# Mixer stage of a decoder on one core: pair products as a ring, residual between the halves of the next block, feed-forward weights split later

## What is computed

```
# long convolution, 32 heads of 8 channels, along the 512 features; ctx is k and v, x is q
kv[i, j] = ctx[i] * ctx[j]                       # 64 products per head, 36 different pairs
y[i, j]  = causal_convolution(kv[i, j], ssm_kernel[head]) + D[head] * kv[i, j]
out[j]   = sum over i of y[i, j] * x[i]
x = layernorm(x + out)
# feed-forward, 512 -> 1408 -> 512
x = layernorm(x + ((silu(x @ gate.T * gate_s) * (x @ up.T * up_s)) @ down.T) * down_s)
```

## Time and profile before

| | us |
|---|---|
| median of 3 runs | 2226.83 (2217.18 to 2228.21) |
| the profiled execution | 2228.92 |
| its span, first to last instruction | 2227.10 |
| PE busy in the span | 1929.4 (87%) |
| DVE busy | 1296.5 (58%) |
| ACT busy | 907.3 (41%) |
| POOL busy | 353.0 (16%) |
| mixer stage, from its first transpose to its last matmul | 624 to 1304 |

### The profile page before, as it was taken

The page is one execution under the profiler, slowest core; times in us unless marked ns, Lnnn a source line. Parts: engine busy times, 40 slices in busy tenths (PEclk is TensorE's granted clock), DMA queues, the critical chain, the costliest instruction groups (busy, mean ns, idle before and its releaser), DMA issues. The chain is left out here.

```text
span 2227.1 us, 32834 instructions
## 1 busy us (share of the span) xinstructions
PE 1929.4 (87%) x11952; PEld 1535.5 (69%) x11952; DVE 1296.5 (58%) x2794; ACT 907.3 (41%) x2264; POOL 353.0 (16%) x508
## 2 busy tenths in 40 slices
PE   6979999999955988998998867899998578888966
PEld 5869998998834887887888855566665345555543
DVE  3446444444436665555565335677776368888847
ACT  2234333333312422222222123656555368788821
POOL 0000000000023222222221011232323311112001
PEclk9989999999967999999999988999999889999988
DMA  2221000000122311110110121000000276554334
GB/s 97 67 85 48 20 20 20 20 20 20 34 81 76 105 34 29 39 43 24 39 29 15 39 76 38 10 29 29 29 20 20 92 201 160 143 146 123 76 117 138
DMA packets 86255, 136.60 MB, mean 61 GB/s; under 512 B 9481, under 2 KB 25481, under 8 KB 86097
## 3 DMA queue, kind: packets, MB, share of 16 engines
q1 hardware_dynamic: 86096, 134.52, 20.6%
HBM read 79.88 MB, written 21.05 MB: 45 GB/s over the span
## 5 line engine op out<-in xcount | busy, mean ns | idle before, releaser
L1142 PE MATMUL yp<-cc,toep 128*128 128x288 f32 x640 | 184.4, 440 | 28.1 <-ACT ring L940 28.1
L1901 ACT ACTIVATE e_p<-e_s_ps,e_nb 128x512 f32<-128x512 f32 x256 | 175.1, 698 | 54.0 <-DVE e_nb L1949 51.8
L1949 DVE TENSOR_REDUCE e_nb<-e_s_ps 128x2 f32<-128x1024 f32 x128 | 155.8, 1218 | 54.7 <-PE e_s_ps L2026 54.0
L1142 PEld LDWEIGHTS yp<-cc,toep 128*128 128x128 f32 x640 | 127.9, 208 | 65.1 <-ACT ring L940 28.4
L2036 PE MATMUL e_t_ps<-ident,e_p 128*128 128x128 f32 x1024 | 148.6, 284 | 24.6 <-DVE e_pT L1956 13.3
L2036 PEld LDWEIGHTS e_t_ps<-ident,e_p 128*128 128x128 f32 x1024 | 120.8, 147 | 62.0 <-issue 52.5
L954 ACT ACTIVATE sg<-gu_ps,gs_col 128x256 f32<-128x256 f32 x88 | 41.7, 474 | 281.5 <-PE gu_ps L82 281.5
L80 PE MATMUL q_ps<-a_xt_hi,wq_hi 128*128 128x256 f32 x512 | 151.8, 297 | 4.1 <-DVE wo_lo L112 4.1
L1415 ACT ACTIVATE p<-p,nb,rq 128x128 f32<-128x128 f32 (+1 forms) x256 | 137.0, 539 | 37.9 <-DVE nb L1513 37.8
L1047 DVE SCALAR_TENSOR_TENSOR hm<-gu_ps,us_col,sg 128x256 f32<-128x256 f32 x88 | 42.3, 481 | 187.7 <-ACT sg L954 187.7
L883 POOL TENSOR_TENSOR cc<-ct 128x224 f32<-128x224 f32 (+6 forms) x224 | 112.7, 538 | 230.8 <-ACT ct L920 195.9
(11 more groups left out here) (270 smaller groups left out, 5266.7 us busy)
## 6 DMA issues: line engine op xcount, KB each, us to landing
x_after<-n_r SPq DMA_DIRECT2D x24, 512.0 KB, 3.0
toep<-padded_kernels SPq DMA_DIRECT2D x32, 256.0 KB, 3.5
qs<-e_xh SPq DMA_DIRECT2D x64, 128.0 KB, 2.5
qs<-e_xl SPq DMA_DIRECT2D x64, 128.0 KB, 2.6
ks<-e_ch SPq DMA_DIRECT2D x64, 128.0 KB, 2.6
ks<-e_cl SPq DMA_DIRECT2D x64, 128.0 KB, 2.6
x<-x_after SPq DMA_DIRECT2D x12, 512.0 KB, 4.6
x<-in_x SPq DMA_DIRECT2D x8, 512.0 KB, 4.0
```

Of the source, the lines that this page charges most:

```text
L1142: last = pe.matmul(yp[:, lo % 2, 0:NCOL], toep[h % 2][:, (lo - li) * P:(lo - li + 1) * P], cc[h % 2][:, li, :], start=(li == 0), stop=(li ...
L1901: act.activation(pr[i][:, a, :], s_ps[i][:, a, :], ACT.Exp, bias=nb[i][:, a:a + 1], accum_out=sums[t][:, j, q:q + 1]).then_inc(e_done, 1)
L1949: dve.tensor_reduce(nb[i][:], s_ps[i][:], AX.X, ALU.max, negate=True).then_inc(nb_done, 1)
```

## The change

- **Ring of pairs.** The pairs of a head are taken round a ring of eight channels: `ct` and `qt` hold their 64 columns twice, so that pair (i, i + d) is a window that starts d channels on. POOL then needs two instructions (distance 4, and distances 1 to 3 in one), ACT squares as before. The 288 columns lie in `ccy`, and PE's matmuls read them as before.
- **Result in place.** `copy_y` writes the convolved columns back into `ccy`, laid out as windows with their continuation (three copies), so there is no `ys`; `copy_y` no longer waits for `pr_done`, and the products and squares of head h wait for the sums of head h - 2 (`ot_done`). So that this is possible, the unit with output blocks 2 and 3 comes first. `terms` are two instructions, `sums` four, and the partial sums beside them are `low`, in the ring tile. `qt` is copied by heads into three buffers.
- **Order.** `heads_at` moves the products of a head one unit pair later, to the tick before its first unit. POOL does `products` before the powers, ACT `squares` before `copy_c`, DVE `sums` before `pair_statistics`.
- **Early residual.** At step 0 of a block PE does the first half of `turn_x`, `down(m-1, 10)`, the second half, and then the unit. DVE does `finish(m-1)`, without its statistics, between the two halves of `lo_x`; the statistics (`block_statistics`) stay in step 1.
- **Later weights.** Six pieces in the opening (at odd ticks), then three in each step of block 0.

```diff
-ct = sb("ct", [P, LB, P])
-qt = [sb(f"qt{k}", [P, LB, P]) for k in range(2)]
+ct = sb("ct", [P, LB, 2, 2, HB])
+qt = [sb("qt0", [P, LB, 2, HB]), sb("qt1", [P, LB, 2, HB]),
+      core.ring[:, 3 * D:4 * D].rearrange("p (k r n) -> p k r n", k=LB, r=2)]
...
-cc = [sb(f"cc{k}", [P, LB, NCOL]) for k in range(2)]
-ys = core.ring[:, 3 * D:3 * D + LB * NCOL].rearrange("p (k n) -> p k n", k=LB)
-pr = sb("pr", [P, HI, LB, HB])
+ccy = [sb(f"ccy{k}", [P, LB, XCOL]) for k in range(2)]
+low = core.ring[:, 4 * D:4 * D + LB * 3 * HB].rearrange("p (k r n) -> p k r n", k=LB, r=3)
...
+def around(tile, first, step, count):
...
+    whole = tile if len(tile.ap) == 3 else tile.rearrange("p k r n -> p k (r n)")
+    start = whole[:, :, first:first + 1]
+    return bass.AP(tensor=start.tensor, offset=start.offset,
+                   ap=[list(start.ap[0]), list(start.ap[1]), [step, count], [1, HB]])
...
 def pieces(m, j, t):
...
     if m is None:
-        return range(t, t + 1)
-    return range(UP + 2 * j, min(UP + 2 * j + 2, len(split.pieces))) if m == 0 else range(0)
+        return range(t // 2, (t + 1) // 2) if t else range(0)
+    return range(UP // 2 + 3 * j, min(UP // 2 + 3 * j + 3, len(split.pieces))) if m == 0 else range(0)
...
 def heads_at(t):
...
-    return (t + 3) // 2 if t % 2 and t <= 2 * HC - 5 else None
+    return (t + 1) // 2 if t % 2 and 3 <= t <= 2 * HC - 3 else None
...
     def _(pool):
         def products(h):
...
+            p = h // 2
+            c, out = ct[:, :, h % 2, :, :], ccy[h % 2]
...
+                pool.wait_ge(ot_done, h - 1)
...
+            pool.tensor_tensor(out[:, :, 0:HB // 2], c[:, :, 0, 0:HB // 2], c[:, :, 0, HB // 2:HB], ALU.mult)
+            pool.tensor_tensor(out[:, :, HB // 2:HB // 2 + 3 * HB].rearrange("p k (r n) -> p k r n", r=3),
+                               around(c, 0, 0, 3), around(c, 5 * B, B, 3), ALU.mult).then_inc(cc_done, 1)
...
         for m, j, t in schedule():
+            if t is not None and heads_at(t):
+                products(heads_at(t))
+            if t is not None and t % 4 == 3 and t >= 7:
+                pair_power((t - 7) // 4)
...
-            if t is not None and t % 4 == 3 and t >= 7:
-                pair_power((t - 7) // 4)
-            if t is not None and heads_at(t):
-                products(heads_at(t))
...
+                act.wait_ge(sq_done, 2 * p)
+            act.activation(ct[:].rearrange("p k h r n -> p (k h) r n"),
+                           tr[:].rearrange("p k (h n) -> p (k h) n", h=2).unsqueeze(2).to_broadcast([P, 2 * LB, 2, HB]),
+                           ACT.Copy).then_inc(c_copied, 1)
...
         def copy_q(p):
...
+            for h in (2 * p, 2 * p + 1):
+                if h >= 3:
+                    act.wait_ge(pr_done, h - 2)
+                half = tr[:, :, h % 2 * HB:h % 2 * HB + HB]
+                act.activation(qt[h % 3][:], half.unsqueeze(2).to_broadcast([P, LB, 2, HB]), ACT.Copy)\
+                   .then_inc(q_copied, 1)
...
         def squares(h):
...
+                act.wait_ge(ot_done, h - 1)
+            act.wait_ge(c_copied, h // 2 + 1)
+            act.activation(ccy[h % 2][:, :, NCOL - HB:NCOL], ct[:, :, h % 2, 0, :], ACT.Square).then_inc(sq_done, 1)
...
         def copy_y(t):
...
-                act.wait_ge(pr_done, h)
...
+            y = ccy[h % 2][:, 2 - 2 * half:4 - 2 * half, :]
+            slots = yp[:, :, HB // 2:NCOL].rearrange("p k (r n) -> p k r n", r=4)
+            act.activation(y[:, :, 0:HB].rearrange("p k (r n) -> p k r n", r=2),
+                           yp[:, :, 0:HB // 2].unsqueeze(2).to_broadcast([P, 2, 2, HB // 2]), ACT.Copy)
+            act.activation(around(y, WIN, WIN, 4), slots, ACT.Copy)
+            act.activation(around(y, WIN + HB, WIN, 3)[:, :, :, 0:EXT], slots[:, :, 0:3, 0:EXT], ACT.Copy)\
+               .then_inc(ys_done, 1)
...
+            if heads_at(t):
+                squares(heads_at(t))
...
-            if heads_at(t):
-                squares(heads_at(t))
...
     def _(dve):
         def terms(h):
...
+            y, q = ccy[h % 2][:], qt[h % 3][:]
...
+            dve.wait_ge(q_copied, h + 1)
+            dve.tensor_tensor(low, around(y, WIN + 3 * B, WIN - B, 3), around(q, 3 * B, -B, 3), ALU.mult)\
+               .then_inc(low_done, 1)
+            dve.wait_ge(low_done, h + 1)
+            dve.tensor_tensor(around(y, 0, WIN, 5), around(y, 0, WIN, 5), around(q, 4 * B, B, 5), ALU.mult)\
+               .then_inc(pr_done, 1)
...
         def sums(h):
...
+            y = ccy[h % 2][:]
+            at = lambda k: y[:, :, k * WIN:k * WIN + HB]
...
+            dve.tensor_tensor(around(y, WIN, WIN, 3), around(y, WIN, WIN, 3), low, ALU.add).then_inc(fold_done, 1)
+            dve.wait_ge(fold_done, 3 * h + 1)
+            dve.tensor_tensor(around(y, WIN, WIN, 2), around(y, WIN, WIN, 2), around(y, 3 * WIN, WIN, 2), ALU.add)\
+               .then_inc(fold_done, 1)
+            dve.wait_ge(fold_done, 3 * h + 2)
+            dve.tensor_tensor(at(1), at(1), at(2), ALU.add).then_inc(fold_done, 1)
+            dve.wait_ge(fold_done, 3 * h + 3)
...
+            dve.tensor_tensor(ot[:, :, base:base + HB], at(0), at(1), ALU.add).then_inc(ot_done, 1)
...
+        def lo_x(m, r):
+            dve.wait_ge(xh_done, 2 * m + r + 1)
+            dve.tensor_tensor(xl[:, 2 * r:2 * r + 2, :], xt_ps[:], xh[:, 2 * r:2 * r + 2, :], ALU.subtract)\
+               .then_inc(xl_done, 1)
...
         def conv(t):
+            if t % 2 and 3 <= t <= NU + 1:
+                sums((t - 3) // 2)
...
-            if t % 2 and 3 <= t <= NU + 1:
-                sums((t - 3) // 2)
...
         for m, j, t in schedule():
...
-                lo_x(m)
+                lo_x(m, 0)
+                if m:
+                    finish(m - 1)
+                lo_x(m, 1)
...
                 if j == 1 and m >= 1:
-                    finish(m - 1)
+                    block_statistics(m - 1)
                 if j == 2 and m >= 1:
...
+        block_statistics(NB - 1)
...
+            for lo in (2 - 2 * half, 3 - 2 * half):
...
         def conv(t):
...
         for m, j, t in schedule():
...
-                turn_x(m)
+                turn_x(m, 0)
+                if m:
+                    down(m - 1, NJ - 1)
+                turn_x(m, 1)
...
-                if m:
-                    down(m - 1, NJ - 1)
```

More of the change, by code:

```diff
@@ L673 @@
 LB = D // P
-RUN = [(HI - d) * B for d in range(HI)]
-OFF = [sum(RUN[:d]) for d in range(HI)]
 HB = HI * B
 PAD = P
+WIN = 12 * B
+EXT = 3 * B
+XCOL = 4 * WIN + HB
 NU = 2 * HC
@@ L783, in l0_mixer @@
         cc_done, sq_done, conv_mm, ys_done = s("cc_done"), s("sq_done"), s("conv_mm"), s("ys_done")
-        pr_done, fold_done, ot_done = s("pr_done"), s("fold_done"), s("ot_done")
+        low_done, pr_done, fold_done, ot_done = s("low_done"), s("pr_done"), s("fold_done"), s("ot_done")
         st2_done, mv2_done, ve2_done, rstd2_done, y2_done = (s(n) for n in (
@@ L937, in copy_y @@
                     act.wait_ge(conv_mm, t + 1)
-                    if h:
-                        act.wait_ge(pr_done, h)
-                    act.activation(ys[:, 2 * half:2 * half + 2, :], yp[:, :, 0:NCOL], ACT.Copy).then_inc(ys_done, 1)
+                    y = ccy[h % 2][:, 2 - 2 * half:4 - 2 * half, :]
[5 more added lines that the diff above has]
+                       .then_inc(ys_done, 1)
                 def round_x(m):
@@ L992, in terms @@
                 def terms(h):
-                    p, base = h // 2, h % 2 * HB
+                    y, q = ccy[h % 2][:], qt[h % 3][:]
                     dve.wait_ge(ys_done, 2 * h + 2)
[L995 to L1005, removed]
@@ L1034, in pair_apply @@
                     dve.tensor_scalar(r, r, mv2[:, 0:1], rstd2[:], ALU.subtract, ALU.mult).then_inc(y2_done, 1)
-                def lo_x(m):
-                    for r in range(2):
-                        dve.wait_ge(xh_done, 2 * m + r + 1)
-                        dve.tensor_tensor(xl[:, 2 * r:2 * r + 2, :], xt_ps[:], xh[:, 2 * r:2 * r + 2, :], ALU.subtract)\
-                           .then_inc(xl_done, 1)
+                def lo_x(m, r):
+                    dve.wait_ge(xh_done, 2 * m + r + 1)
+                    dve.tensor_tensor(xl[:, 2 * r:2 * r + 2, :], xt_ps[:], xh[:, 2 * r:2 * r + 2, :], ALU.subtract)\
+                       .then_inc(xl_done, 1)
                 def gated(m, j):
@@ L1062, in finish, with block_statistics @@
                         dve.tensor_tensor(r[:, t, :], d_ps[t][:], r[:, t, :], ALU.add).then_inc(added, 1)
+                def block_statistics(m):
+                    r = xb[m % 3]
                     for t in range(T):
@@ L1139, in unit @@
                         pe.wait_ge(ys_done, t)
-                    for lo in (2 * half, 2 * half + 1):
+                    for lo in (2 - 2 * half, 3 - 2 * half):
                         for li in range(lo + 1):
                             last = pe.matmul(yp[:, lo % 2, 0:NCOL], toep[h % 2][:, (lo - li) * P:(lo - li + 1) * P],
```

(21 more changed lines are left out.)

20 lines of the change are left out of this document (removed).

## The result

The changed kernel takes 2190.32 us (median; 2188.10 to 2192.86) against 2223.30 before (2217.18 to 2228.21) on the same chip: ratio 0.985, 95% interval 0.982 to 0.988. The forecast was 2181 us, in a range of 2166 to 2199; of the 46 us that it promised, 33 came. The span of the profiled execution fell from 2227.1 to 2191.0 us.

The account below looks back on a forecast made before the run. TensorE, busy 87% of the span, was taken as the bound, so only its gaps and slow clock could be won: 29.7 + 14.1 + 3.0 - 0.7 = 46.1 us off the 2226.8 us median gave 2181 us, range 2166 to 2199.

Parts of the forecast that it names:

- Early residual: At the seven passages between blocks: PE's idle time falls by 29.7 us, and the clock staying fast wins 14.1 us.
- Products late: In the blocks: POOL's later products stay covered by PE's other work, by 0.8 us at step 0; cost nothing.
- Prices of the ring: Durations forecast for the new pair instructions: `terms` 2.4, `sums` 2.5, `products` 2.3, `copy_y` about 1.05 us.
- surcharge of 1.0 us: In the opening: extra time for each of three of five heads whose `terms` run beside `products`, 1.0 us each.
- Opening: From unit 0 on: `gate_up(0,0)` comes at about 723.4 instead of 726.4, 3 us won.
- Later weights: Block 0, three pieces per step: loads arrive in time; only step 3, where ACT's squares come late, costs 0.7 us.
- (a): Rival at the passages: the wait only moves, small gaps still slow the clock, the 14.1 us stay; 2195 us, chance 0.12.
- (b): Rival in the opening: no long gap any more, units run at the full clock; 2169 us, chance 0.10.
- (c): Rival in the opening: it becomes longer, 17 us by its upper prices; 2201 us, chance 0.06.
- (d): Rival at unit 2h: late, large `products` hold up PE; 2261 us if they take 8; chance 0.04 with other slower cases.
- (e): Rival at the passage: the wait stays because `hl` holds `down(m-1,10)`; excluded beyond 0.4 us, no chance given.
- signs: Right: PE idle 1 to 2 us per block, opening 85 to 98; wrong: PE waits on `lo_x` or products, blocks 1 to 6.

Follow-up runs that it names:

- e2: Kernel before the change with the early residual alone, old pairs and old weight placing; 2175.6 us, ratio 0.980.
- e11: Changed kernel with fourteen weight pieces in even opening units, none in steps 3 and 8 of block 0, `finish` behind both `lo_x` halves; 2156.2 us, ratio 0.969.
- e4: Changed kernel with twelve weight pieces in the opening, two per even unit from unit 2, and two per step of block 0; 2163.9 us, ratio 0.974.
- e7: Changed kernel without the loads of weight pieces 9 to 32 and ACT's waits for them; 2180.0 us, one run.
- e12: Changed kernel with five slots for loaded weight pieces instead of three, all transfers kept; 2183.3 us, ratio 0.981.
- e3: Changed kernel without the early residual, ring and later weights kept; 2212.7 us, ratio 0.995.
- e1: Changed kernel with weight pieces placed as before, one per opening unit and two per step of block 0; 2181.6 us, ratio 0.982.

## Why the prediction came out as it did

- **Early residual: right.** From `gate_up(1,0)` on 42.8 us came for 43.8 forecast, with gaps of 0.15 to 0.25 for 0.4, and of 0.84 us (once 1.28) for 0.7, and 2.74 at block 7. The clock held in all seven passages, where six and a half were counted. The gap beside the short unit of step 0 was in the forecast; not foreseen was that the long unit of the old pairs leaves none there (e2).
- **Products late, "cost nothing": right.** No unit of blocks 1 to 6 waits for POOL. The 0.8 us of cover was real: e11 spent it, and the wait appeared.
- **Prices of the ring: right alone, wrong together.** `sums` took 2.5 us as forecast, `copy_y` about 0.95 for 1.05, `products` 2.26 (0.45 + 1.81) for 2.3. Beside `terms` my surcharge of 1.0 us was mis-sized:

```profile
647.91 0.95 DVE L1013 TENSOR_TENSOR ring<-ccy,qt 128x768 f32<-128x768 f32 x1
648.07 1.10 POOL L891 TENSOR_TENSOR ccy<-ct 128x128 f32<-128x128 f32 x1 [18.52 <-DVE ot L1033]
648.89 1.62 DVE L1016 TENSOR_TENSOR ccy<-ccy,qt 128x1280 f32<-128x1280 f32 x1
649.13 3.04 POOL L892 TENSOR_TENSOR ccy<-ct 128x768 f32<-128x768 f32 x1
652.23 5.13 PE L1164 MATMUL yp<-ccy,toep 128*128 128x288 f32 x14 [5.78 <-POOL ccy L892]
```

  POOL pays 1.10 + 3.04 - 2.26 = 1.9 us; DVE's rows stay at 0.95 and go from 1.49 to 1.62. Both times DVE began first. The Trainium skill (SBUF — State Buffer, "Who interferes with whom") says that the issue order decides which of the two is blocked, and for the whole instruction. The trace agrees: held until the two instructions of `terms` end at 648.86 and 650.51, POOL's two would end at 649.32 and 652.32; they ended at 649.17 and 652.17. The 1.9 us lie between the 1.0 of the sum and the 2.4 that the prediction worked out by the rule, which fits with `products` beginning 0.16 us behind `terms` and their first instruction going between the two of `terms`. I had set the rule aside because both engines pay in the earlier trace rows; there, 15 short instructions met 7.
- **Opening: right in sum, by luck** (91.2 us for 91.8). From unit 0 to unit 12 it took 78.7 us for 77.4, with the larger surcharge in it; from there to `gate_up(0,0)` 12.6 us for 14.4. The two errors cancel. What another placing of the pieces is worth, 19.5 us (e4), I did not see: I costed the pieces by their number, not by what stands behind them.
- **Later weights, "block 0 cost 0.7 us": the step that failed.** It cost 12.0 us. The line "a load lands in 2.8 us, and SP issues it a step (4.3 us or more) ahead of its use" failed in both halves. The lead: with three slots a load can't be issued before the piece in its slot was taken, and at step 3 that was 2.0 us before ACT was ready, not 4.3. The landing time: 2.8 us is that of a load in the opening; three loads and a row of `x` in one burst had ACT waiting until 2.95 to 4.27 us after the issue. Had each landed in 2.8 us, ACT would have stood about 0.9 us there, an estimate from these rows; it stood 2.2. e7 and e12 put 8.2 and 8.3 us of the block on lateness; 3.7 are left to engine work. These 12 us are the difference between forecast and result: 46.1 - 11.3 = 34.8, against 36.1 of the spans (33 of the medians).
- **Rivals.** (a) fell: the clock is 1.00 behind the small gaps. (b) fell: the long units of heads 2 to 6 took 5.1 to 6.6 us. (c) did not occur: the opening got 3.6 us shorter, though its surcharge came nearer to 2.4 than to 1.0; its 2201 counts the 17 us from the opening before, and from the sum's own it would be 2198. (d) did not occur: POOL's large instruction took 3.05 us at most. (e) was rightly excluded. None of the rivals and none of the signs looked at block 0. The 2190.3 us lie just above the 2173 to 2190 that went with the forecast alone, and inside the wide range only because that was drawn for other causes, (a), (b) and (c), none of which came: in part luck.

Open: 0.4 of the 1.3 us by which the ring's blocks are longer than those of e2; idle time of PE (1.0 us in block 2 for 0.15) explains the rest. Open too is why one gap of 2.47 us in e3 brought the slow clock and four of 2.45 to 2.46 did not. The ring alone, without the other parts, was not run.

## What to carry over

Cost a load by the burst in which it travels and by the slot that it waits for; the shortest step between issue and use decides, not the mean one. Ask of each small piece of work not how long it takes but which chain stands behind it in its engine's order: six pieces in odd units went with an opening of 91.2 us, twelve in even ones with one of 71.7, both on the ring. Test the parts of a change one by one: here two parts removed in part the same loss, and one of them was worth less than nothing as placed.

## What was not expected of the hardware

A large instruction of POOL beside one of DVE that began before it took 3.04 us for 1.81, and DVE's 1.62 for 1.49: as short instructions the two had shared the loss (about 1 us each), as long ones the later paid nearly all. e1 has the other order: there `take_lo` of DVE began 0.51 us behind POOL's 1.81 us and took 1.84 us for 0.69, and POOL paid nothing.

And the length of one gap did not settle the clock. In e3 it stayed at 1.00 behind four gaps of 2.45 to 2.46 us, but fell to 0.62 behind one of 2.47; in block 0 of the changed kernel it fell to 0.50 behind 1.34 and 2.24 us, and in the earlier trace rows to 0.61 behind 4.18. What makes the difference, no run here shows.
